# Masked stage: the two score products of a slot issued in turn; rotary stage: value products two units at a time instead of four

## The chip, the cores and the metric

The kernel runs on one core of a Trainium2 chip. The time is that of one execution on the device, in microseconds (us). A core has TensorE (matrix products, PE in the rows, with PEld for its weight loads), VectorE (DVE), ScalarE (ACT), GpSimd (POOL) and SyncE (SP, which issues the DMA transfers here). Each runs its own list of instructions in order and waits for the others by semaphores.

## The reference

Four attention layers, each followed by a small dense layer, on x of shape (4, 1024, 128), with 16 heads of 8 columns. Each layer gives one stage of the kernel, with 64 heads (4 batches x 16).

```
MASKED: q, k, v = norm(x) @ Wqkv + b;  p = softmax(q k^T / sqrt(8), keys >= query);  x += (p v) @ Wo + bo
RBF:    p = exp(-sigma * |k_i - q_j|^2), no softmax;                                 x += (p v) @ Wproj + b
REL:    softmax of (q k^T + relative positions, shifted) / sqrt(8);                  x += (p v) @ Wo + bo
ROPE:   q, k turned by their position (rotary);  softmax(q k^T / sqrt(8));           x += (p v) @ Wo + bo
after each: x += dense(norm(x))
```

For one head, p has 1024 x 1024 elements. The change touches the heads of MASKED and of ROPE.

## The kernel before

**Rounds and slots.** The kernel runs one round per head n, from n = -2 on. In round n two things are made side by side: the transposed scores S^T of head n (keys on the partitions, called kq), whose exponentials are needed for the values, and the scores S of head n + 2 (queries on the partitions, called qk), of which only the maximum of each row is wanted. A round has slots u = 0, 1, 2, ...; a slot makes one unit of each side, that is, up to four 128 x 128 tiles in one PSUM bank of 512 columns. `KQ_UNITS` and `QK_UNITS` name the tiles: a masked head has 9 units, since half of its tiles are hidden, a rotary head 16. A unit is a list of pieces (row tile, first column tile, tiles, place in the bank). In the masked stage the units of slots 3, 5 and 8 have two pieces on either side (3 + 1, 2 + 2 and 3 + 1 tiles), each with a tile on the diagonal; the others have one.

**The engines in a slot.** TensorE: `unit_kq` (its product is line 821 for MASKED and ROPE) and then `unit_qk` (line 866). The contraction has 51 rows on partitions 64 to 114 for kq and 48 rows on partitions 0 to 47 for qk, so each uses one half of the array's rows. In a diagonal tile two small products of 64 rows (line 826 for kq, `hide_kq`; line 871 for qk, `hide_qk`) add -1e30 to what is hidden; I call them masking steps. ScalarE takes the kq bank and writes its exponential into one of eight `probs` buffers (line 1043). VectorE reduces the qk bank to maxima `mx` (lines 1155 and 1166). Each side has three banks of `ring`: a kq product waits until the exponential of three units ago is out (`s_exp`), a qk product until the maxima of three items ago are (`s_sm`).

**The maximum's way.** After the last slot VectorE reduces `mx` to `mall` (line 1184), GpSimd splits it in three bf16 parts (lines 1401 to 1407), TensorE turns them (line 881, `turn_max`, after slot 3 of the masked rounds and slot 5 of the rotary ones), VectorE copies them to `mrow` (line 1194) and SyncE moves them to the rows of `qst` (line 616) that the next round's first kq product needs (`s_ldm`).

**Values.** `take_values` (line 909) multiplies the values with the exponentials of one unit into `ppv`, one f32 product for each tile, on a quarter of the array's columns; four tiles in different quarters run side by side. The trace shows two matmuls for each. `lag` says which units pass at which slot; slots past the end lie in the next round. A masked head passes three units at slots 5, 8 and 11, a rotary head four units at slots 5, 9, 13 and 17. The same rule serves the last two heads of the RBF stage.

**Fills.** In some rounds the TensorE list holds projections and transposes for the next batch or the end of the last one (`starts`, `finishes`, into `pm`, lines 925 to 995), at the slots that `Plan` sets. `Plan` isn't changed. Of the 64 rotary rounds 30 have fills; of the masked rounds 1 to 61, 37 run at the shortest interval.

Of the kernel before, what the change touches and what calls it, by code (L numbers as in the profile page):

```python
# [15 lines left out]
P = 128  # L16
NT = T // P
HALF = 512
SLOTS = 4
STAGES = 4  # L20
MASKED, RBF, REL, ROPE = range(STAGES)
HEADS = B * H
# [8 lines left out]
BASE = 6 * D  # L31
ROW = P // 2
# [30 lines left out]
def stage(n):  # L63
    return n // HEADS
# [11 lines left out]
def soft_index(n):  # L76

    return n - (HEADS if stage(n) > RBF else 0)
# [58 lines left out]
def loads_to(n):  # L137

    return 16 * sum(NLOAD[stage(m)] for m in range(n % SLOTS, n + 1, SLOTS))


def places_to(n):

    return 16 * sum(NPLACE[stage(m)] for m in range(n % SLOTS, n + 1, SLOTS))


def lag(rd):

    n = len(rd.kq)
    if rd.wide:  # L150
        return {u + 3: [u, u + 1] for u in range(0, n, 2)}
    if rd.s == REL:
        return {6: [0, 1, 2, 3, 4], 10: [5, 6, 7, 8], 14: [9, 10, 11, 12], 19: [13, 14, 15, 16, 17]}
    if n == 9:
        return {5: [0, 1, 2], 8: [3, 4, 5], 11: [6, 7, 8]}
    return {u + 5: [u, u + 1, u + 2, u + 3] for u in range(0, n, 4)}


def values_at(n, u):

    out = []
    if 0 < n <= LAST:
        out += [(n - 1, v) for v in lag(ROUNDS[n - 1]).get(u + ROUNDS[n - 1].slots, [])]
    if 0 <= n < LAST:
        out += [(n, v) for v in lag(ROUNDS[n]).get(u, []) if u < ROUNDS[n].slots]
    return out
# [203 lines left out]
def build(nc, a, k, out):  # L370
# [9 lines left out]
    with ctx:  # L380
        def sb(name, shape, dt=F32):
            return ctx.enter_context(nc.sbuf_tensor(name, shape, dt))

        def ps(name, shape):
            return ctx.enter_context(nc.psum_tensor(name, shape, F32))

        def sem(name):
            return ctx.enter_context(nc.semaphore(name))
# [56 lines left out]
        halves = sb("halves", [P, 2, P], BF16)  # L445
        hide_qk = sb("hide_qk", [P, 2, P], BF16)
        hide_kq = sb("hide_kq", [P, 2, P], BF16)
# [6 lines left out]
        ring = ps("ring", [P, 6, HALF])  # L454
# [9 lines left out]
        s_ld = [sem(f"s_ld{i}") for i in range(SLOTS)]  # L464
        s_ldm = [sem(f"s_ldm{i}") for i in range(SLOTS)]
        s_vs = [sem(f"s_vs{i}") for i in range(SLOTS)]
        s_os = [sem(f"s_os{i}") for i in range(SLOTS)]
        s_st = sem("s_st")
        s_exp = sem("s_exp")
        s_pv = sem("s_pv")  # L470
        s_ev = sem("s_ev")
        s_s = sem("s_s")
        s_sm = sem("s_sm")
# [29 lines left out]
        def rowset(s):  # L503

            return kst[s % 2], qst[s % 2]

        def bank_kq(rd, u):
            if rd.wide:
                y = 2 * (((rd.n - HEADS) * NT + u) % 3)
                return ring[:, y:y + 2]  # L510
            return ring[:, 3 + (rd.narrow + u) % 3]
# [257 lines left out]
        def _(pe):  # L769
# [60 lines left out]
            def unit_qk(rd, u):  # L830
# [41 lines left out]
                                               stop=end and h == 1)  # L872
                mm.then_inc(s_s, 1)

            def turn_max(rd):

                pe.wait_ge(s_mp, 4 * (soft_index(rd.n + 1) + 1))
                item = rd.turned()
                if item >= 3:
                    pe.wait_ge(s_sm, item - 2)  # L880
                pe.transpose(ring[:, item % 3].bitcast(BF16)[0:3 * NT, 0:P], mparts[:, (rd.n + 1) % 2].rearrange("p a t -> p (a t)"),
                             identb[:, :]).then_inc(s_s, 1)
# [89 lines left out]
            def finishes():  # L972

                for f in range(INTERVALS):
                    s, j = f // B, interval_of(f)
                    for h in range(2):
                        name = ("fill", j, f, "wo", h)
                        yield AT[name]
                        filled(name)
                        if s == RBF:  # L980
                            pe.wait_ge(s_ot, 64 * (f + 1))
                        else:
                            pe.wait_ge(s_at, soft_before(f) + 1)
                        for t in range(4):
                            q = (2 * t + h) * P
                            mm = pe.matmul(pm[:, t * P:(t + 1) * P], oT[:, q:q + P], wo[:, s], start=True, stop=True)  # L986
                        mm.then_inc(s_pf, 1)
                    yield from turn_norm(j, f, "f", f, "tf")
                    for h in range(2):
                        name = ("fill", j, f, "ff", h)  # L990
                        yield AT[name]
                        filled(name)
                        pe.wait_ge(s_wf, 2)
                        for t in range(4):
                            mm = pe.matmul(pm[:, t * P:(t + 1) * P], xnT[:, (4 * h + t) * P:(4 * h + t + 1) * P], wf[:, s // 2],  # L995
                                           start=True, stop=True)
                        mm.then_inc(s_pf, 1)
# [3 lines left out]
            start, finish = Steps(starts()), Steps(finishes())  # L1001
            start.go(-1)
            for rd in ROUNDS.values():
                if rd.n == 0:
                    pe.wait_ge(s_c1, NC1[0])
                for u in range(rd.slots):
                    if u < len(rd.kq):
                        unit_kq(rd, u)
                    if u < len(rd.qk):
                        unit_qk(rd, u)  # L1010
                    if u == rd.turn:
                        turn_max(rd)
                    for n, v in values_at(rd.n, u):
                        take_values(n, v)
                    start.go(rd.tick + u)
                    finish.go(rd.tick + u)
# [663 lines left out]
```

## Time and profile before

| | |
|---|---|
| median of 3 runs | 3001.47 us (3000.57 to 3001.97) |
| the profiled execution's own time | 2993.65 us |
| its span, first to last instruction | 2991.9 us |
| mean granted TensorE clock | 0.989 |
| busy: PE, PEld, DVE, ACT, POOL | 93%, 58%, 69%, 71%, 25% |
| chain that ended last | PE 74%, DVE 14%, ACT 4%, issue 4% |

The masked stage lies from about 70 to 602 us, RBF to 1127, REL to 2171, ROPE to 2950. Busy shares of TensorE count a matmul from its start to its modelled end, some 0.17 us after its last column went in, so rows that overlap are common: pace is read from start to start. "Idle before" in brackets is time in which the engine ran nothing, with what ended it.

### The profile page before, as it was taken

What the parts mean: (1) busy time and instruction counts of PE and PEld (TensorE: products, weight loads), DVE (VectorE), ACT (ScalarE), POOL (GpSimd) and SP (SyncE); (2) the same over time, 40 slices, a digit from 0 to 9 for tenths busy, and PEclk for the clock granted to TensorE, in tenths of its full rate; (3) what the DMA queues carried; (4) which work ended last, traced back from release to release, by engine and by line L of the source; (5) the groups of instructions that cost most, each with busy time, mean ns of one, the idle gap of its engine ahead of it and who ended that gap; (6) DMA issues with size and microseconds to landing.
All of it is one profiled execution on the core that took longest, in us unless ns stands there. A gap on an engine that the chain in (4) does not pass through costs nothing.

```text
span 2991.9 us, 106514 instructions
## 1 busy us (share of the span) xinstructions
PE 2779.5 (93%) x43980; PEld 1722.2 (58%) x44112; DVE 2076.9 (69%) x4755; ACT 2135.0 (71%) x3793; POOL 753.8 (25%) x1369
## 2 busy tenths in 40 slices
PE   4999999999999999999999999899988898888885
PEld 2677676755555556666666666566544444444443
DVE  3887787731221247777787777777789989889893
ACT  1676666789999986666666666566677777777773
POOL 3212222331312424401611440140032140231101
PEclk9999999999999999999999999999999999999997
DMA  5323232343323342311321231221113221132211
GB/s 173 96 78 112 79 110 74 111 137 94 114 80 118 96 134 63 114 47 52 103 66 47 69 110 47 68 76 56 37 53 94 61 80 57 55 94 60 75 52 31
DMA packets 195708, 244.78 MB, mean 82 GB/s; under 512 B 47044, under 2 KB 113220, under 8 KB 195224
## 3 DMA queue, kind: packets, MB, share of 16 engines
q1 hardware_dynamic: 195224, 237.96, 27.0%
q8 instruction: 349, 5.72, 0.8%
q14 instruction: 135, 1.11, 0.1%
HBM read 133.77 MB, written 100.14 MB: 78 GB/s over the span
## 4 chain that ended last, share of the span: by engine, by line
PE 74%; DVE 14%; ACT 4%; issue 4%; SPq 1%; DMA 1%; POOL 1%; ACTq 0%; DVEq 0%; POOLq 0%
PE ppv L909 30%; DVE mx L1166 9%; PE ring L821 8%; PE ring L810 6%; PE ring L859 5%; PE ring L794 5%; PE pm L941 3%; ACT probs L1043 3%; PE ring L866 3%; PE ring L826 2%; PE ring L850 2%; DVE seen L1161 1%; PE ring L871 1%; PE pm L986 1%; PE pm L995 1%
## 5 line engine op out<-in xcount | busy, mean ns | idle before, releaser
L1043 ACT ACTIVATE probs<-ring 128x512 f32<-128x512 f32 (+1 forms) x3280 | 1986.4, 697 | 787.8 <-PE ring L821 348.6
L1166 DVE TENSOR_REDUCE mx<-ring 128x1 f32<-128x512 f32 (+2 forms) x2112 | 1291.7, 649 | 287.0 <-PE ring L866 117.0
L909 PE MATMUL ppv<-probs,values 128*32 128x128 f32 x30208 | 1102.2, 277 | 5.6 <-DVE osb L1175 2.7
L909 PEld LDWEIGHTS ppv<-probs,values 128*32 128x32 f32 x30208 | 808.5, 110 | 245.3 <-issue 130.3
L866 PE MATMUL ring<-kst,qst 48*128 48x512 bf16 (+3 forms) x1792 | 563.1, 365 | 39.7 <-DMA kst<-records_k 20.6
L821 PE MATMUL ring<-qst,kst 51*128 51x512 bf16 (+4 forms) x1824 | 538.5, 362 | 37.0 <-ACT probs L1043 31.5
L1161 DVE CUSTOM_DVE_ANT_0 seen<-ring,low_seen 128x512 f32<-128x512 f32 x576 | 393.2, 683 | 138.1 <-PE ring L859 137.5
L1401 POOL CAST mparts<-mall 128x8 bf16<-128x8 f32 x192 | 36.7, 191 | 1310.2 <-DVE mall L1184 1303.1
L821 PEld LDWEIGHTS ring<-qst,kst 51*128 51x128 bf16 (+1 forms) x1824 | 137.3, 94 | 276.8 <-ACT probs L1043 171.6
L859 PE MATMUL ring<-kst,qst 112*128 112x512 bf16 (+3 forms) x768 | 251.0, 327 | 0.9 <-DVE mx L1166 0.9
L810 PE MATMUL ring<-qst,kst 115*128 115x512 bf16 (+3 forms) x768 | 250.6, 326 | 0.1
L866 PEld LDWEIGHTS ring<-kst,qst 48*128 48x128 bf16 x1792 | 145.6, 94 | 112.0 <-DVE mx L1166 57.2
L810 PE MATMUL ring<-qst_up,kst 115*128 115x512 bf16 (+3 forms) x640 | 205.0, 320 | 0.0
L859 PE MATMUL ring<-kst,qst_up 112*128 112x512 bf16 (+3 forms) x640 | 201.3, 315 | 2.4 <-DVE mx L1161 2.3
L1175 DVE COPY osb<-ppv 128x256 f32<-128x256 f32 x64 | 27.2, 424 | 238.3 <-PE ppv L909 238.3
L794 PE MATMUL ring<-qst,kst 54*128 54x512 bf16 x992 | 171.7, 385 | 0.0
L871 PE MATMUL ring<-hide_qk,halves 64*128 64x128 bf16 x1024 | 127.8, 220 | 0.0
L826 PE MATMUL ring<-hide_kq,halves 64*128 64x128 bf16 x1024 | 125.3, 217 | 0.0
L813 PE MATMUL ring<-low_kq,identb 128*128 128x129 bf16 (+2 forms) x576 | 123.8, 215 | 0.0
L826 PEld LDWEIGHTS ring<-hide_kq,halves 64*128 64x128 bf16 x1024 | 93.5, 96 | 41.2 <-issue 1.3
L810 PEld LDWEIGHTS ring<-qst_up,kst 115*128 115x128 bf16 x640 | 62.3, 97 | 89.1 <-issue 39.7
L810 PEld LDWEIGHTS ring<-qst,kst 115*128 115x128 bf16 x768 | 74.8, 97 | 52.6 <-issue 15.3
(143 smaller groups left out, 2687.2 us busy)
## 6 DMA issues: line engine op xcount, KB each, us to landing
qst<-records_q SPq DMA_DIRECT2D x448, 96.0 KB
heads_out<-osb SPq DMA_DIRECT2D x256, 128.0 KB, 1.9
kst<-records_k SPq DMA_DIRECT2D x320, 96.0 KB
records_k<-parts SPq DMA_DIRECT2D x96, 256.0 KB, 3.3
records_q<-parts SPq DMA_DIRECT2D x96, 256.0 KB, 3.5
kst<-records_k SPq DMA_DIRECT2D x128, 102.0 KB
oT<-heads_out SPq DMA_DIRECT2D x64, 128.0 KB, 2.7
den<-inverses SPq DMA_DIRECT2D x48, 128.0 KB, 2.6
```

The costliest lines, as they stand in the source:

```text
L794: mm = pe.matmul(bank[:, h], keys[rows, slot, kt * P:(kt + 1) * P], qs[rows, slot, h * HALF:(h + 1) * HALF], start=True, stop=True)
L810: mm = pe.matmul(bank[:, p0 - lo:p1 - lo], keys[rows, slot, kt * P:(kt + 1) * P], qq[rows, slot, p0:p1], start=p0 == lo, stop=p1 == hi and ...
L813: mm = pe.matmul(bank[:, m0 - lo:m1 - lo], identb[:, :], low_kq[:, m0 - first:m1 - first], start=False, stop=True)
L821: mm = pe.matmul(bank[:, at * P:(at + nt) * P], keys[rows, slot, kt * P:(kt + 1) * P], qs[rows, slot, q0 * P:(q0 + nt) * P], start=i == 0, ...
L826: mm = pe.matmul(bank[:, c:c + P], halves[half, h], hide_kq[half, h], start=False, stop=end and h == 1)
L859: mm = pe.matmul(bank[:, p0 - lo:p1 - lo], qq[rows, slot, qt * P:(qt + 1) * P], keys[rows, slot, p0:p1], start=p0 == lo, stop=p1 == hi)
L866: mm = pe.matmul(bank[:, at * P:(at + nt) * P], qs[rows, slot, qt * P:(qt + 1) * P], keys[rows, slot, k0 * P:(k0 + nt) * P], start=i == 0, ...
L871: mm = pe.matmul(bank[:, c:c + P], halves[half, h], hide_qk[half, h], start=False, stop=end and h == 1)
L909: mm = pe.matmul(ppv[32 * g:32 * g + 32, c:c + P], values[:, (n // H) % 2, v:v + 32], src[:, at * P:(at + 1) * P], start=u == 0 and qt < 4 ...
L1043: nc.scalar.activation(probs_of(rd.n, u), src, ACT.Exp, scale=1.0 if rd.s == RBF else SCALE).then_inc(s_exp, 1)
L1161: dve.tensor_tensor_reduce(seen[:, item % 3], bank[:, :], low_seen[:, first:first + HALF], 1.0, 3.0 * BIG, ALU.add, ALU.max, mx[:, slot, ( ...
L1166: ins = dve.tensor_reduce(mx[:, slot, to:to + 1], bank[:, at * P:(at + nt) * P], AX.X, ALU.max)
```

## The change

Two edits. First, in masked rounds 1 to 61 a new function `unit_both` takes the place of `unit_kq` and `unit_qk`: piece by piece it issues the kq product, then the qk product, then the masking steps of the two in turn. The waits are those of before; the wait for the qk bank (`s_sm`) stands between the first kq product and the first qk product. Second, `lag` for heads of 16 units passes units 0, 1 at slot 5, units 2, 3 at slot 6, and from unit 4 on the pair u, u + 1 at slot u + 4, so 8 passes of two units instead of 4 of four.

```
-    return {u + 5: [u, u + 1, u + 2, u + 3] for u in range(0, n, 4)}
+    return {5: [0, 1], 6: [2, 3], **{u + 4: [u, u + 1] for u in range(4, n, 2)}}
...
+            def unit_both(rd, u):
...
+                if u == 0:
+                    pe.wait_ge(s_ldm[n % SLOTS], places_to(n))
+                    pe.wait_ge(s_ld[m % SLOTS], loads_to(m))
+                if e >= 3:
+                    pe.wait_ge(s_exp, e - 2)
...
+                for i in range(max(len(rd.kq[u]), len(rd.qk[u]))):
+                    if i < len(rd.kq[u]):
...
+                        mm = pe.matmul(scores[:, at * P:(at + nt) * P], keys[ROW:ROW + BASE + 3, n % SLOTS, kt * P:(kt + 1) * P],
+                                       qs[ROW:ROW + BASE + 3, n % SLOTS, q0 * P:(q0 + nt) * P], start=i == 0, stop=end and not hidden)
...
+                    if i == 0 and item >= 3:
+                        pe.wait_ge(s_sm, item - 2)
+                    if i < len(rd.qk[u]):
...
+                        mm = pe.matmul(tops[:, to * P:(to + mt) * P], qs_m[0:BASE, m % SLOTS, qt * P:(qt + 1) * P],
+                                       keys_m[0:BASE, m % SLOTS, k0 * P:(k0 + mt) * P], start=i == 0, stop=end_m and not hidden_m)
...
+                    for h in range(2):
+                        if i < len(rd.kq[u]) and hidden:
+                            mm = pe.matmul(scores[:, c:c + P], halves[high, h], hide_kq[high, h], start=False, stop=end and h == 1)
...
+                        if i < len(rd.qk[u]) and hidden_m:
+                            mm = pe.matmul(tops[:, cm:cm + P], halves[low, h], hide_qk[low, h], start=False, stop=end_m and h == 1)
...
-                    if u < len(rd.kq):
-                        unit_kq(rd, u)
-                    if u < len(rd.qk):
-                        unit_qk(rd, u)
+                    if 0 < rd.n < HEADS - 2:
+                        unit_both(rd, u)
```

TensorE in a masked round, slot 3 and the turn of the maxima behind it. The rows name line, operation, output and inputs, and the output's size; `qst`, `kst` are the two operands, `ring` the banks. Before:

```order
L821 MATMUL ring<-qst,kst 128x384
L826 MATMUL ring<-hide_kq,halves 128x128 x2
L821 MATMUL ring<-qst,kst 128x128
L826 MATMUL ring<-hide_kq,halves 128x128 x2
L866 MATMUL ring<-kst,qst 128x384
L871 MATMUL ring<-hide_qk,halves 128x128 x2
L866 MATMUL ring<-kst,qst 128x128
L871 MATMUL ring<-hide_qk,halves 128x128 x2
L881 MATMUL ring<-identb,mparts 24x128
```

The same place in the changed kernel:

```order
L892 MATMUL ring<-qst,kst 128x384
L902 MATMUL ring<-kst,qst 128x384
L908 MATMUL ring<-hide_kq,halves 128x128
L912 MATMUL ring<-hide_qk,halves 128x128
L908 MATMUL ring<-hide_kq,halves 128x128
L912 MATMUL ring<-hide_qk,halves 128x128
L892 MATMUL ring<-qst,kst 128x128
L902 MATMUL ring<-kst,qst 128x128
L908 MATMUL ring<-hide_kq,halves 128x128
L912 MATMUL ring<-hide_qk,halves 128x128
L908 MATMUL ring<-hide_kq,halves 128x128
L912 MATMUL ring<-hide_qk,halves 128x128
```

The turn (L922) follows. The qk products moved up from behind all kq instructions to right behind the kq product of the same piece.

TensorE in a rotary round, from slot 5 with the turn to the next passes. Before, with four units (16 tiles) a pass:

```order
L821 MATMUL ring<-qst,kst 128x512
L866 MATMUL ring<-kst,qst 128x512
L881 MATMUL ring<-identb,mparts 24x128
L909 MATMUL ppv<-probs,values 32x128 x16
L821 MATMUL ring<-qst,kst 128x512
L866 MATMUL ring<-kst,qst 128x512
L821 MATMUL ring<-qst,kst 128x512
L866 MATMUL ring<-kst,qst 128x512
```

And in the changed kernel:

```order
L821 MATMUL ring<-qst,kst 128x512
L866 MATMUL ring<-kst,qst 128x512
L922 MATMUL ring<-identb,mparts 24x128
L950 MATMUL ppv<-probs,values 32x128 x8
L821 MATMUL ring<-qst,kst 128x512
L866 MATMUL ring<-kst,qst 128x512
L950 MATMUL ppv<-probs,values 32x128 x8
L821 MATMUL ring<-qst,kst 128x512
L866 MATMUL ring<-kst,qst 128x512
```

The pass of units 0 to 3 is cut in two, and slot 6's products moved between the halves; further on a pass stands behind every second slot. The lists of the other engines keep their order.

## Rows read from the trace of the kernel before

**Rows 1.** Windows, masked and rotary stage: us, busy by engine, clock, DMA

```profile
81.00:595.00 514.00, 505.04 (x8182) 358.77 (x8180) 408.42 (x921) 355.49 (x697) 133.84 (x313) 1.00 0.33 95
...
2171.00:2950.00 779.00, 687.91 (x10637) 368.45 (x10635) 671.97 (x1276) 594.94 (x1193) 172.36 (x336) 0.99 0.23 66
```

**Rows 2.** Timeline of TensorE, plain masked round: start, us, line, tiles, count

```profile
300.26 0.33 PE L821 MATMUL ring<-qst,kst 51*128 51x384 bf16 x1
...
300.51 0.33 PE L866 MATMUL ring<-kst,qst 48*128 48x384 bf16 x1
300.55 0.22 PE L821 MATMUL ring<-qst,kst 51*128 51x128 bf16 x1
...
301.06 0.23 PE L881 MATMUL ring<-identb,mparts 128*24 128x128 bf16 x1
...
301.98 0.28 PE L866 MATMUL ring<-kst,qst 48*128 48x256 bf16 x1
...
302.52 0.86 PE L909 MATMUL ppv<-probs,values 128*32 128x128 f32 x24
303.32 0.39 PE L821 MATMUL ring<-qst,kst 51*128 51x512 bf16 x1
```

**Rows 3.** The same timeline, slot 7 and the start of slot 8

```profile
303.55 0.38 PE L821 MATMUL ring<-qst,kst 51*128 51x512 bf16 x1
303.55 0.38 PE L866 MATMUL ring<-kst,qst 48*128 48x512 bf16 x1
303.76 0.22 PE L826 MATMUL ring<-hide_kq,halves 64*128 64x128 bf16 x1
...
303.88 0.32 PE L821 MATMUL ring<-qst,kst 51*128 51x384 bf16 x1
```

**Rows 4.** Timeline of VectorE, slot 3 of the same round

```profile
301.16 0.75 DVE L1166 TENSOR_REDUCE mx<-ring 128x1 f32<-128x384 f32 x2 [0.33 <-PE ring L871]
```

**Rows 5.** Waits of VectorE, 81 to 589 us: us in sum, times, longest

```profile
DVE mx L1166 <- PE ring L871: 64.4, 119, 1.9
DVE mx L1166 <- PE ring L866: 25.8, 62, 0.5
```

**Rows 6.** Windows: a plain masked, a plain rotary, a rotary round with projections

```profile
300.26:307.73 7.47, 7.47 (x131) 5.44 (x130) 6.17 (x14) 5.19 (x11) 0.78 (x4) 1.00 0.25 73
...
2330.23:2340.92 10.69, 9.73 (x165) 5.26 (x162) 10.12 (x19) 8.54 (x17) 0.78 (x4) 1.00 0.18 51
...
2400.30:2414.90 14.60, 12.67 (x141) 5.18 (x138) 9.63 (x17) 10.60 (x21) 0.96 (x5) 1.00 0.10 30
```

**Rows 7.** Timeline of VectorE, plain rotary round

```profile
2334.63 3.67 DVE L1166 TENSOR_REDUCE mx<-ring 128x1 f32<-128x512 f32 x6
2338.22 0.20 DVE L1194 COPY mrow<-ring 24x128 bf16<-24x128 bf16 x1
2338.85 3.82 DVE L1166 TENSOR_REDUCE mx<-ring 128x1 f32<-128x512 f32 x6 [0.42 <-PE ring L866]
```

**Rows 8.** Timeline of TensorE, same round: scores, values of four units, scores

```profile
2331.43 0.39 PE L866 MATMUL ring<-kst,qst 48*128 48x512 bf16 x1
2331.75 1.08 PE L909 MATMUL ppv<-probs,values 128*32 128x128 f32 x32
2332.76 0.39 PE L821 MATMUL ring<-qst,kst 51*128 51x512 bf16 x1
```

**Rows 9.** Timeline of TensorE, slot 5 of a masked round behind a transpose

```profile
219.42 0.27 PE L821 MATMUL ring<-qst,kst 51*128 51x256 bf16 x1
...
219.59 0.28 PE L866 MATMUL ring<-kst,qst 48*128 48x256 bf16 x1
```

**Rows 10.** Timeline of TensorE, rotary round with projections

```profile
2408.57 0.39 PE L821 MATMUL ring<-qst,kst 51*128 51x512 bf16 x1
...
2408.89 1.12 PE L941 MATMUL pm<-xnT,wkp 128*128 128x512 f32 x2
2409.95 0.39 PE L821 MATMUL ring<-qst,kst 51*128 51x512 bf16 x1
```

More of the change, by code:

```diff
@@ L873, in unit_qk @@
                 mm.then_inc(s_s, 1)
+            def unit_both(rd, u):
+                n, m = rd.n, rd.n + 2
+                e, item = rd.exps + u, rd.maxes + u + (0 <= rd.turn < u)
+                (keys, qs), (keys_m, qs_m) = rowset(stage(n)), rowset(stage(m))
+                if u == 0:
[3 more added lines that the diff above has]
+                    pe.wait_ge(s_exp, e - 2)
+                low, high = slice(0, ROW), slice(ROW, P)
+                scores, tops = bank_kq(rd, u), ring[:, item % 3]
+                for i in range(max(len(rd.kq[u]), len(rd.qk[u]))):
+                    if i < len(rd.kq[u]):
+                        kt, q0, nt, at = rd.kq[u][i]
+                        end, hidden = i == len(rd.kq[u]) - 1, q0 <= kt < q0 + nt
+                        c = (at + kt - q0) * P
+                        mm = pe.matmul(scores[:, at * P:(at + nt) * P], keys[ROW:ROW + BASE + 3, n % SLOTS, kt * P:(kt + 1) * P],
+                                       qs[ROW:ROW + BASE + 3, n % SLOTS, q0 * P:(q0 + nt) * P], start=i == 0, stop=end and not hidden)
+                        if end and not hidden:
+                            mm.then_inc(s_st, 1)
+                    if i == 0 and item >= 3:
+                        pe.wait_ge(s_sm, item - 2)
+                    if i < len(rd.qk[u]):
+                        qt, k0, mt, to = rd.qk[u][i]
+                        end_m, hidden_m = i == len(rd.qk[u]) - 1, k0 <= qt < k0 + mt
+                        cm = (to + qt - k0) * P
+                        mm = pe.matmul(tops[:, to * P:(to + mt) * P], qs_m[0:BASE, m % SLOTS, qt * P:(qt + 1) * P],
+                                       keys_m[0:BASE, m % SLOTS, k0 * P:(k0 + mt) * P], start=i == 0, stop=end_m and not hidden_m)
+                        if end_m and not hidden_m:
+                            mm.then_inc(s_s, 1)
+                    for h in range(2):
+                        if i < len(rd.kq[u]) and hidden:
+                            mm = pe.matmul(scores[:, c:c + P], halves[high, h], hide_kq[high, h], start=False, stop=end and h == 1)
+                            if end and h == 1:
+                                mm.then_inc(s_st, 1)
+                        if i < len(rd.qk[u]) and hidden_m:
+                            mm = pe.matmul(tops[:, cm:cm + P], halves[low, h], hide_qk[low, h], start=False, stop=end_m and h == 1)
+                            if end_m and h == 1:
+                                mm.then_inc(s_s, 1)
@@ L1006, in _ @@
                 for u in range(rd.slots):
-                    if u < len(rd.kq):
-                        unit_kq(rd, u)
-                    if u < len(rd.qk):
-                        unit_qk(rd, u)
+                    if 0 < rd.n < HEADS - 2:
+                        unit_both(rd, u)
+                    else:
+                        if u < len(rd.kq):
+                            unit_kq(rd, u)
+                        if u < len(rd.qk):
+                            unit_qk(rd, u)
                     if u == rd.turn:
```

## The prediction

> **What bounds the kernel now.** Read first the windows by stage [rows 1]: TensorE counts as busy for 505 of 514 us in the masked stage and for 688 of 779 us in the rotary stage. Matmul ends are modelled and each matmul's 0.2 us of latency is counted, so these shares say only that TensorE is hardly ever empty. What it does with the time is read from its timeline, start to start.
>
> A masked head without projection work takes 7.47 us: the 384-column product of slot 3 starts at 300.26 and again at 307.73, which is a window of [rows 6]. I call such a round plain. Its parts on TensorE follow without a hole, except one wait in slot 5. Score products use one half of the array each: S^T (kq) the upper 64 rows, S (qk) the lower 64. In slot 7 both run together: L821 and L866 start at 303.55, their two masking steps each from 303.76 on, and slot 8 starts at 303.88 [rows 3]; a paired masking step is thus 0.06 us. In slot 3 they don't: L821 starts at 300.26, but L866, which stands behind six kq instructions, at 300.51 [rows 2]. TensorE does look past some of them (the 128-column kq product, ahead of L866 in the order, starts at 300.55), yet not past all, and the lower half is empty for 0.25 us. VectorE stands idle in front of each of slots 0, 3 and 6, with 0.33 us before slot 3 [rows 4], and for 90 us in sum over 61 heads [rows 5]. So TensorE sets the pace of a plain masked round and VectorE has room.
>
> A plain rotary round is 10.69 us (window of 2330.23 to 2340.92), with VectorE at 10.12 us [rows 6]. Six row maxima in a row take 3.67 us, so the pitch is (3.67 - 0.68) / 5 = 0.598 us [rows 7]; 16 of them, a copy of 0.20 and a reduction and its gap of some 0.20 make 9.97 us. VectorE lacks 0.72 us per round: 0.42 behind the turned maximum [rows 7], and 0.1 us or so behind each of the other value passes, which the timeline merges into its runs (six maxima in 3.82 us instead of 3.67). All of them lie where TensorE runs a block of values of four units, 1.01 us from its start to the next score product (2331.75 to 2332.76) [rows 8].
>
> **The masked edit.** It changes the order of instructions on TensorE alone; none is added. Slot by slot:
> - Slots 0, 1, 2, 4, 6, 7 have one piece a side. Slot 0 keeps its order, and in slots 1 and 7 both halves are full already. Nothing.
> - Slot 3, and slot 8 of the same shape. Now: 0.25 (late start of qk) + 0.46 (384 columns 0.17, 128 columns 0.06, four masking steps 0.23) + 0.09 (change to the whole array for the turn) = 0.80, which is 300.26 to 301.06 [rows 2]. Then: both start together, 0.46 + 0.09 = 0.55. Saved: 0.25 us in each.
> - Slot 5. Its L866 starts at 301.98, 0.07 after VectorE has finished slot 3's maxima (301.16 + 0.75 = 301.91) [rows 2, 4]: it waits for that bank. This wait stays and now also holds the kq masking steps behind it. But VectorE started at 301.16 because slot 3's last qk masking step, L871, had ended (the releaser in its row), and that is 0.25 earlier afterwards. From L866 to the values it is 0.54 us, and the paired order needs no more. So the values of slot 5 come earlier by the 0.25 that slot 3 saved, and no second gain is there.
>
> A plain round is worth 0.25 + 0.25 = **0.50 us**. What is late next: VectorE starts slot 3 with 0.33 us of idle time before it [rows 4]; 0.08 is left. It is busy 6.17 of 7.47 us [rows 6], so 6.97 us still holds it. The kq result of slot 5 comes some 0.3 us later in its slot; ScalarE is busy 5.19 us of the round and no value pass needs slot 5 before slot 8. The load for the next head and the maximum's way over GpSimd keep their order; their distances shrink by 0.25 us.
>
> The edit holds in 61 heads. Going by the intervals from one slot 3 to the next, 37 are plain: 37 x 0.50 = 18.5 us. In 11 TensorE does projections or transposes and waits for nobody; there slot 5 has no wait, and its qk product starts 0.17 late (219.42 and 219.59) [rows 9], so 0.25 + 0.25 + 0.17 = 0.67 each, 7.4 us. In the other 13 a wait for ScalarE, a transfer or VectorE's squares is on the path and takes half of it: 13 x 0.2 = 2.6 us. Together **28 us**, bounds 15 (VectorE or the waits take half) and 33.
>
> The Trainium skill, "TensorE: Matmul & The Clock Gate", Part 3, says that matmuls are strictly first in, first out and only weight loads are pulled ahead. The trace differs: L866 at 300.51 runs before kq steps that stand ahead of it. By the page's rule slot 3 would have taken 2 x 0.46 + 0.09 = 1.01 us and the edit would give 0.46 per slot; the row has 0.80, and the sum goes by the row.
>
> **The rotary edit.** Before, units 0 to 3 pass at slot 5, then four units every four slots; after, two units at slots 5 and 6 and then every two slots. 64 heads, and the last two of the Gaussian stage, which I leave at nothing. The newest unit of a pass is then 3 slots old (4 at slot 5) instead of 2, so no pass waits longer for its exponential.
> - Price: a value block costs more than its matmuls. Three units take 0.80 (302.52 to 303.32) [rows 2] and four 1.01 [rows 8], so a unit is 0.21 and the block 0.16 on top; entering it costs 0.1 (L866 at 2331.43, values at 2331.75, with 0.22 of columns) [rows 8]. Two units take 0.58. Eight blocks instead of four: 4 x 0.26 = 1.04 us more of TensorE per head.
> - Gain: the longest stretch without scores falls from 1.01 to 0.58.
> In a plain round TensorE's own work is 16 x 0.22 = 3.5 for score pairs, 16 x 0.21 = 3.4 for values, now 4 x 0.26 = 1.0 and then 2.1, and 0.2 for the turn: 8.1 and then 9.2 us, under VectorE's 9.97. So the price is hidden behind VectorE, and the 0.42 of idle time behind the turn is covered by the 0.43 that the block is shorter. Between 0 and 0.72 I take 0.35, half, since TensorE then has only 0.8 us to spare and every pair still waits for two engines. 32 plain rounds x 0.35 = **11 us** saved.
> The other 32 heads: in two no maxima are computed, nothing counted. In 30 there are projections; around 2408 values, scores and a projection of 1.06 us follow each other with no wait [rows 10]. There each extra block costs its 0.26, up to 1.04 per head. But the window of such a round has TensorE busy only 12.67 of 14.60 us [rows 6]; the rest is waits for ScalarE and banks, which shorter blocks fill. I take 0.1 lost per head, **3 us**, bounds 30 lost and 10 won.
>
> **Sum.** 2993.65 (the profiled execution's own time, 1.75 more than its span) - 28 - 11 + 3 = 2957.7. The median of the runs is 3001.47, 7.8 above; with it, 2965.5.
>
> **Rivals.**
> - Rotary neutral or worse (0.12): TensorE paces the 30 fill rounds, which lose most of 1.04 us each, and the plain rounds gain nothing or little: -28 + 20 = -8, 2993. For it: [rows 10] without a hole. Against: the 1.9 us of waits in such a round.
> - VectorE takes over the masked rounds (0.13): 0.08 us of room before slot 3 is thin; if it isn't there, a plain round gains only 0.25: -15 - 11 + 3 = -23, 2978.
> - More (0.08): the rotary rounds reach VectorE's floor (32 x 0.72 = 23) and the fill rounds gain 8: -28 - 23 - 8 = -59, 2942.
> - Slower (0.07): the extra block changes pace the whole rotary stage. It decides once TensorE's sum passes VectorE's 9.97 us, that is, if a block change costs over 0.36 instead of 0.26. Then 64 rounds pay 1.04 or more: +67 - 28 = +39, 3040. Against it: two independent block lengths give the same 0.16.
> - The edits not in effect (under 0.01): the order on TensorE shows both.
>
> **How the numbers follow.** The forecast, 2965.5, has 0.60; masked 20 to 33 us and rotary 0 to 18 us give 2950 to 2981. With the rivals on either side in part, the range is 2945 to 2990. A measurement of this kernel can't tell 0.2% (6 us) from no change. Faster by more: 0.60 + 0.13 + 0.08 and half of the first rival, 0.86. Within: the other half and small remains, 0.07. Slower: 0.07.
>
> **What would show it.** In the trace after: both 384-column products of slots 3 and 8 start together; a plain masked round of 6.97 us (7.2 means VectorE, 7.47 nothing won); slot 5's qk product still starts just after slot 3's maxima. A plain rotary round of 10.3 us, eight value blocks of 0.58 with no idle time of VectorE behind the turn; fill rounds within 0.3 us of now. Wrong would be: pairs that start together and yet last longer than 0.06 a step, or rotary rounds above 10.69.

## The result: 1.4% faster

The changed kernel takes 2960.91 us (median of 4 executions, 2954.58 to 2967.66). The kernel before took 3001.72 us beside it. The ratio is 0.9862, with a 95% interval of 0.9832 to 0.9893. The predicted 2965.5 us lies 4.6 us above the measured median. The profiled execution took 2954.58 us (its span is 2952.8), 39.07 less than that of before. Of the executions behind the figures further below, two, one of the late turn (3661.42 us, mean granted clock 0.659) and one of the kernel before beside the last kernel (3495.26 us, 0.730), lie hundreds of us above all others and are left out of the medians and ratios.

Measured from the end of the first exponential of each stage's first head to that of the next stage (in the rotary stage to the end of its last exponential), these 39 us lie as follows (us, profiled executions):

| stage | before | after | difference | of it, by kind of round |
|---|---|---|---|---|
| masked | 532.4 | 510.5 | -21.9 | 37 plain -15.3, 11 fill rounds -6.5, 13 others -0.6, first round +0.5 |
| Gaussian | 524.2 | 524.5 | +0.3 | its last round +0.3 |
| relative | 1044.3 | 1047.7 | +3.4 | its first round +0.5, the rest in rounds with projections and transfers |
| rotary | 778.6 | 757.8 | -20.8 | 32 plain -13.5, 30 fill rounds -5.9, last two -1.4 |

A stage's sum holds to about 3 us only: stages that an edit leaves alone move by that much from one profile to the next (next section).

First the windows of the trace after: the masked and the rotary stage, a plain masked round and a plain rotary one (columns as in [rows 1] and [rows 6]: length, then busy us of TensorE, its weight loads, VectorE, ScalarE, GpSimd, then clock and DMA).

```profile
81.00:567.00 486.00, 458.85 (x8086) 307.99 (x8085) 407.23 (x912) 350.16 (x687) 130.66 (x307) 0.99 0.34 99
2130.00:2910.00 780.00, 721.62 (x10895) 344.40 (x10886) 682.51 (x1300) 624.31 (x1217) 173.24 (x341) 0.99 0.22 67
268.94:275.95 7.01, 6.71 (x130) 4.58 (x130) 6.16 (x14) 5.17 (x11) 0.78 (x4) 1.00 0.56 157
2324.05:2334.32 10.27, 9.76 (x165) 4.63 (x162) 10.03 (x19) 8.86 (x17) 0.78 (x4) 1.00 0.19 56
```

The masked round is 7.01 us where it was 7.47, the rotary one 10.27 where it was 10.69 [rows 6]. VectorE has the same work in both (6.16 and 6.17 us; 10.03 and 10.12 us): it stands idle for less.

TensorE's timeline of slots 3 to 5, the counterpart of [rows 2]:

```profile
268.94 0.33 PE L892 MATMUL ring<-qst,kst 51*128 51x384 bf16 x1
268.94 0.33 PE L902 MATMUL ring<-kst,qst 48*128 48x384 bf16 x1
...
269.34 0.21 PE L912 MATMUL ring<-hide_qk,halves 64*128 64x128 bf16 x1
269.49 0.23 PE L922 MATMUL ring<-identb,mparts 128*24 128x128 bf16 x1
...
269.87 0.27 PE L892 MATMUL ring<-qst,kst 51*128 51x256 bf16 x1
270.44 0.28 PE L902 MATMUL ring<-kst,qst 48*128 48x256 bf16 x1 [0.30 <-DVE mx L1210]
...
270.99 0.86 PE L950 MATMUL ppv<-probs,values 128*32 128x128 f32 x24
```

Both products of slot 3 start at 268.94, and the turn follows after 0.55 us, where it was 0.80. Slot 5's S product still waits, now by 0.30 us, for VectorE's maxima of slot 3. These are the three instructions of VectorE before that wait ends, the last of slot 2 and both of slot 3 (compare [rows 4]):

```profile
268.82 0.68 DVE L1210 TENSOR_REDUCE mx<-ring 128x1 f32<-128x512 f32 x1
269.62 0.56 DVE L1210 TENSOR_REDUCE mx<-ring 128x1 f32<-128x384 f32 x1
270.10 0.28 DVE L1210 TENSOR_REDUCE mx<-ring 128x1 f32<-128x128 f32 x1
```

VectorE ends slot 2 at 269.50 and starts slot 3 at 269.62. The 0.33 us of idle time before slot 3 are 0.12 now. Slot 3's maxima start 0.68 us after its products, where it was 0.90 (301.16 - 300.26 in [rows 4] and [rows 2]), so they come 0.22 earlier in the slot. TensorE alone would have made it 0.25: from the last masking step's modelled end (269.34 + 0.21) to the reduction it is 0.07 us. Slot 8 takes 0.54 us from its first product to the values behind it:

```profile
272.34 0.32 PE L892 MATMUL ring<-qst,kst 51*128 51x384 bf16 x1
272.34 0.32 PE L902 MATMUL ring<-kst,qst 48*128 48x384 bf16 x1
...
272.88 1.28 PE L950 MATMUL ppv<-probs,values 128*32 128x128 f32 x24
```

In the kernel before it was 0.78, from the 303.88 of [rows 3] to

```profile
304.66 1.28 PE L909 MATMUL ppv<-probs,values 128*32 128x128 f32 x24
```

VectorE's waits for scores in the masked stage (us in sum, times, longest) are 65 us in the lines that answer to [rows 5], where they were 90:

```profile
DVE mx L1210 <- PE ring L912: 40.3, 78, 2.0
DVE mx L1210 <- PE ring L902: 24.6, 62, 0.5
```

In the plain rotary round (VectorE's timeline, as in [rows 7]) only one idle stretch of 0.20 us is left behind the turned maximum:

```profile
2327.68 0.20 DVE L1238 COPY mrow<-ring 24x128 bf16<-24x128 bf16 x1
2327.88 0.69 DVE L1210 TENSOR_REDUCE mx<-ring 128x1 f32<-128x512 f32 x1
2328.78 5.47 DVE L1210 TENSOR_REDUCE mx<-ring 128x1 f32<-128x512 f32 x9 [0.20 <-PE ring L866]
```

Nine maxima in 5.47 us are a pitch of (5.47 - 0.68) / 8 = 0.599 us: VectorE's own, without a gap. TensorE, on the other side, now waits for VectorE twice around the turn, before the S product of slot 5 and before the turn itself (its timeline):

```profile
2324.35 0.65 PE L950 MATMUL ppv<-probs,values 128*32 128x128 f32 x16
2324.93 0.39 PE L821 MATMUL ring<-qst,kst 51*128 51x512 bf16 x1
...
2326.03 0.39 PE L866 MATMUL ring<-kst,qst 48*128 48x512 bf16 x1 [0.21 <-DVE mx L1210]
2326.72 0.22 PE L922 MATMUL ring<-identb,mparts 128*24 128x128 bf16 x1 [0.30 <-DVE mx L1210]
```

A block of two units is 0.58 us from its start to the next scores (2324.35 to 2324.93), as predicted.

### The profile page after: what moved, and what is told of

It reads as the page before. It is cut to its first block, busy times and chain, and to the rows that moved or that the text cites. A ratio compares the mean times of both kernels' runs of the same rounds, so it can differ in the third digit from the quotient of the medians.

```text
span 2952.8 us, 106453 instructions
## 1 busy us (share of the span) xinstructions
PE 2754.6 (93%) x43980; PEld 1641.9 (56%) x44112; DVE 2073.6 (70%) x4755; ACT 2150.1 (73%) x3793; POOL 753.2 (26%) x1369
## 4 chain that ended last, share of the span: by engine, by line
PE 68%; DVE 20%; issue 5%; ACT 3%; SPq 1%; DMA 1%; POOL 1%; ACTq 0%; DVEq 0%; POOLq 0%
PE ppv L950 28%; DVE mx L1210 15%; PE ring L810 6%; PE ring L859 6%; PE ring L794 5%; PE ring L821 3%; PE ring L892 3%; PE pm L982 3%; PE ring L850 2%; DVE seen L1205 1%; ACT probs L1087 1%; PE pm L1027 1%; PE ring L908 1%; PE pm L1036 1%; ACT xn L1095 1%
## 5 line engine op out<-in xcount | busy, mean ns | idle before, releaser
L950 PE MATMUL ppv<-probs,values 128*32 128x128 f32 x30208 | 1156.9, 278 | 5.6 <-DVE osb L1219 2.7
L950 PEld LDWEIGHTS ppv<-probs,values 128*32 128x32 f32 x30208 | 791.9, 110 | 334.0 <-issue 181.3
L866 PE MATMUL ring<-kst,qst 48*128 48x512 bf16 (+1 forms) x1060 | 366.3, 391 | 43.1 <-DVE mx L1210 21.4
L821 PE MATMUL ring<-qst,kst 51*128 51x512 bf16 (+2 forms) x1092 | 346.6, 385 | 3.6 <-ACT probs L1087 3.0
L902 PE MATMUL ring<-kst,qst 48*128 48x512 bf16 x732 | 210.5, 330 | 16.5 <-DVE mx L1210 16.5
L892 PE MATMUL ring<-qst,kst 51*128 51x512 bf16 x732 | 203.6, 329 | 3.7 <-DMA qst<-mrow 3.7
L1219 DVE COPY osb<-ppv 128x256 f32<-128x256 f32 x64 | 27.2, 424 | 238.7 <-PE ppv L950 238.7
L866 PEld LDWEIGHTS ring<-kst,qst 48*128 48x128 bf16 x1060 | 90.8, 94 | 122.5 <-DVE mx L1210 76.6
L821 PEld LDWEIGHTS ring<-qst,kst 51*128 51x128 bf16 (+1 forms) x1092 | 70.9, 94 | 138.3 <-ACT probs L1087 95.8
L912 PE MATMUL ring<-hide_qk,halves 64*128 64x128 bf16 x976 | 118.6, 216 | 0.0
```

The lines of the kernel that those rows point to most:

```text
L821: mm = pe.matmul(bank[:, at * P:(at + nt) * P], keys[rows, slot, kt * P:(kt + 1) * P], qs[rows, slot, q0 * P:(q0 + nt) * P], start=i == 0, ...
L866: mm = pe.matmul(bank[:, at * P:(at + nt) * P], qs[rows, slot, qt * P:(qt + 1) * P], keys[rows, slot, k0 * P:(k0 + nt) * P], start=i == 0, ...
L892: mm = pe.matmul(scores[:, at * P:(at + nt) * P], keys[ROW:ROW + BASE + 3, n % SLOTS, kt * P:(kt + 1) * P], qs[ROW:ROW + BASE + 3, n % SLO ...
L902: mm = pe.matmul(tops[:, to * P:(to + mt) * P], qs_m[0:BASE, m % SLOTS, qt * P:(qt + 1) * P], keys_m[0:BASE, m % SLOTS, k0 * P:(k0 + mt) * ...
L950: mm = pe.matmul(ppv[32 * g:32 * g + 32, c:c + P], values[:, (n // H) % 2, v:v + 32], src[:, at * P:(at + 1) * P], start=u == 0 and qt < 4 ...
```

## The experiments

Eleven kernels ran. All diffs are against the changed kernel. Stage and round times come from each kernel's profiled execution, by the ends of the heads' first exponentials, as in the table above; "plain round" is the median over the plain ones. Ratios are to the kernel before, on the same chip; the changed kernel's is 0.9862 (0.9832 to 0.9893).

### The two edits apart

The masked edit alone, rotary passes as before:

```
-    return {5: [0, 1], 6: [2, 3], **{u + 4: [u, u + 1] for u in range(4, n, 2)}}
+    return {u + 5: [u, u + 1, u + 2, u + 3] for u in range(0, n, 4)}
```

> The masked edit alone; the rotary stage passes four units at a time as before. My reading (each edit works in its own stage): the masked stage loses 22 us and the rotary stage keeps 778.6 us, so about 2971 us profiled, 22 below the kernel before. Rival (the masked edit is worth less alone, part of the gain is a shift of work between the stages): less than 15 us. In the profile a plain masked round of 7.02 us and a plain rotary round of 10.69 us.

Measured: 2969.86 us, ratio 0.9896 (0.9879 to 0.9913). Plain masked round 7.02 us, plain rotary round 10.70; rounds 127 and 128 take 15.5 and 14.6 us as before, where the changed kernel has 15.8 and 15.1.

The rotary edit alone:

```
-                    if 0 < rd.n < HEADS - 2:
+                    if False:
```

> The rotary edit alone; masked slots as before. My reading: masked stage 532 us as before, rotary stage 758 us, so 21 us below the kernel before, 32 plain rounds giving 13.5 us, the two last rounds 1.5 us and the rounds with projections 6 us. Rival (rotary neutral, block changes eat it): within 6 us of the kernel before. In the profile plain rotary rounds of 10.27 us.

Measured: 2990.02 us, ratio 0.9948 (0.9927 to 0.9969). Plain masked round 7.46 us, plain rotary 10.27. The two ratios multiply to 0.9845, and the changed kernel has 0.9862: **the edits add**, within the intervals. Each plain round moves with its own edit alone. The stage sums are less sharp. The masked edit alone left the masked stage at 507.5 us and the rotary stage, whose order it doesn't touch, at 775.4, where before has 778.6; the rotary edit alone has 529.8 us for the untouched masked stage (532.4 before) and 761.4 for the rotary one. The median with the rotary edit alone is 13.8 us below the kernel before beside it and not the 21 expected; its executions spread from 2978.70 to 3000.79 us, and the profiled one, the longest, ran 54 us at half clock (last section).

### What gates slot 5

The prediction said that slot 5's wait for VectorE stays and that slot 5's own pairing is worth nothing in a plain round, but 0.17 us in a fill round. Slot 5 as before, the rest paired:

```
-                    if 0 < rd.n < HEADS - 2:
+                    if 0 < rd.n < HEADS - 2 and u != 5:
```

> The changed kernel, but slot 5 of the masked rounds issues all kq products first and then the qk products, as before. My reading (in a plain round slot 5 waits for VectorE to finish slot 3's maxima, whatever the order): plain masked rounds stay at 7.02 us within 0.03; the 11 rounds with a projection lose 0.1 to 0.17 us each. Rival (the paired order in slot 5 carries part of the gain): plain rounds at 7.15 or more. A second rival (the pairing holds slot 5's masking steps back behind the wait and costs): plain rounds below 6.99.

Measured: plain masked round 7.017 us, which is unchanged; the 11 fill rounds 108.8 us in sum, where the changed kernel has 106.9. That is 0.17 each on average (0.15 to 0.19), the upper end of what was expected. The total of one execution (2968.19 us) says little: 23.9 us of it ran at half clock (last section).

Then a part of VectorE's work in front of that wait is left out: the second maximum of slot 3 (128 columns, 0.28 us, of which 0.20 lie behind the end of the first). The row maxima of one tile are missing from the result.

```
-                    for qt, k0, nt, at in unit:
+                    for qt, k0, nt, at in unit[:1] if u == 3 and stage(n) == MASKED and n > 2 else unit:
```

> The changed kernel, but VectorE leaves out the 128-column maximum of slot 3 (one tile's row maxima are not computed), 0.28 us less work per masked round, for heads 3 to 63. My reading (VectorE gates slot 5, and this gate is what the masked edit runs into): slot 5's qk product starts up to 0.2 us earlier and a plain masked round takes 6.8 us. Rival (TensorE alone sets the round, VectorE's time is hidden): 7.02 us as without it.

Measured: plain masked round 6.820 us, 0.197 less; the stage 498.9 us. The 11 fill rounds, in which slot 5 waits for nobody, stayed at 106.9 us. VectorE stands idle for parts of every round, 6.16 of 7.01 us being busy, and still 0.2 us less of it shortens the round by 0.2. It isn't the bound by its sum, but **slot 3's maxima are on the path** of a plain round.

### Slot 8

```
-                    if 0 < rd.n < HEADS - 2:
+                    if 0 < rd.n < HEADS - 2 and u != 8:
```

> The changed kernel with slot 8 of every round issued as before (all of the S^T product's steps, then the S product's). Theory: TensorE paces the end of the masked round, so slot 8 takes 0.78 us instead of 0.54 and a plain masked round 7.26 us; the stage is 61 x 0.24 = 15 us longer at most and 9 at least (the plain rounds alone). Rival (VectorE paces the whole round since the edit): 7.02 to 7.08 us.

Measured: plain masked round 7.255 us, 0.237 more, and each of the 11 fill rounds 0.24 more; the stage 519.0 us, 8.5 more, just short of the least expected (9), its first round being 1.3 us shorter here. TensorE's timeline in slot 8 shows the old stagger:

```profile
269.73 0.32 PE L821 MATMUL ring<-qst,kst 51*128 51x384 bf16 x1
...
269.96 0.33 PE L866 MATMUL ring<-kst,qst 48*128 48x384 bf16 x1
270.00 0.22 PE L821 MATMUL ring<-qst,kst 51*128 51x128 bf16 x1
...
270.50 1.28 PE L950 MATMUL ppv<-probs,values 128*32 128x128 f32 x24
```

Slot 8 takes 0.77 us here and 0.54 paired. Its gain is TensorE's own and arrives whole. No kernel has slot 3 apart: what is left of the plain round's 0.44 us is 0.20.

### The place of the turn

Slot 5 waits because the S banks go round in three and the turn, at slot 3, takes one of them: slot 5's bank is the one that slot 3 filled. With the turn behind slot 5, slot 5 gets the bank of slot 2, and the turn itself has to wait for slot 3's maxima. The same number also moves VectorE's copy of the turned maxima and SyncE's load of them by two slots.

```
-TURN_SLOT = [3, 0, 6, 5]
+TURN_SLOT = [5, 0, 6, 5]
```

> The changed kernel, with the turned maximum of the masked rounds behind slot 5 instead of slot 3. Slot 5's qk product then no longer waits for slot 3's maxima, since one item fewer stands between them. My reading (VectorE's gate costs a plain masked round up to 0.4 us): 6.6 to 6.85 us per plain round, 6 to 15 us in all. Rival (the later copy of the maxima makes the next round's first kq product wait for its transfer, which takes 2 us from the copy): plain rounds of 7.0 us or more, with waits of L892 for qst<-mrow.

Measured: 2953.99 us (median of four executions), ratio 0.9833 (0.9811 to 0.9855), which can't be told from the changed kernel's; plain masked round 6.687 us, 0.33 less than the changed kernel; the stage 496.4 us, 14.1 less. Of these, 11.6 us lie in the 37 plain rounds and 3.6 in the stage's first round: it took 9.8 to 11.6 us in the ten kernels with the turn at slot 3 and 7.7 to 8.5 in the three with a later turn, and why wasn't looked into. The 13 rounds that are neither plain nor fill rounds took 1.8 more. TensorE's timeline, slot 5 and the turn, then slot 8 and the next slot 0:

```profile
262.57 0.27 PE L892 MATMUL ring<-qst,kst 51*128 51x256 bf16 x1
262.57 0.27 PE L902 MATMUL ring<-kst,qst 48*128 48x256 bf16 x1
...
263.48 0.21 PE L922 MATMUL ring<-identb,mparts 128*24 128x128 bf16 x1 [0.31 <-DVE mx L1210]
263.61 0.86 PE L950 MATMUL ppv<-probs,values 128*32 128x128 f32 x24
...
264.96 0.32 PE L892 MATMUL ring<-qst,kst 51*128 51x384 bf16 x1
...
265.50 1.28 PE L950 MATMUL ppv<-probs,values 128*32 128x128 f32 x24
266.72 0.39 PE L892 MATMUL ring<-qst,kst 51*128 51x512 bf16 x1
```

Slot 5's products start together. A wait of 0.31 us remains, but it stands behind slot 5's scores and no longer ahead of them. The price shows in the waits of the first S^T product of a round for the load of the maxima (us in sum, times, longest), of its weights (PEld) and of the product itself (PE). First the changed kernel, then this one:

```profile
PEld ring L892 <- DMA qst<-mrow: 4.2, 2, 2.3
PE ring L892 <- DMA qst<-mrow: 3.7, 2, 2.0
```

```profile
PEld ring L892 <- DMA qst<-mrow: 15.1, 45, 2.2
PE ring L892 <- DMA qst<-mrow: 5.4, 6, 1.9
```

The weights' 2 waits have become 45, the product's 2 have become 6: the load now lands just in time. The two rows lie over each other in time and don't add. One slot later still:

```
-TURN_SLOT = [3, 0, 6, 5]
+TURN_SLOT = [6, 0, 6, 5]
```

> The changed kernel with the turn of the maxima in the masked rounds at slot 6, two slots of one piece after slot 5's bank. Theory: at slot 5 the turn still waits 0.3 us for VectorE in each round, but its result then reaches the next head's operands just in time (waits for the load of the maxima, 20 us in sum). One slot later the first is smaller and the second larger: plain masked rounds 6.7 to 7.0 us, and the waits of the first S^T product for the load grow beyond 20 us. Rival (the load has slack, the turn's wait is what is left): 6.4 to 6.6 us.

Measured: 2969.12 us (one execution); plain masked round 7.26 us, beyond the upper end of what I had expected; the stage 522.0 us. The same two waits:

```profile
PEld ring L892 <- DMA qst<-mrow: 27.8, 47, 1.9
PE ring L892 <- DMA qst<-mrow: 15.8, 45, 1.6
```

They grew, as the theory had it: the weights' by 12.7 us over 61 rounds, 0.21 each, and 45 products wait where 6 did. The round lost 0.57. The rest is in slot 8: slot 6, the turn and slot 7 have the three banks ahead of it, so it waits for slot 6's maximum as slot 5 did for slot 3's (TensorE's timeline of this kernel):

```profile
270.00 0.32 PE L892 MATMUL ring<-qst,kst 51*128 51x384 bf16 x1
...
270.46 0.33 PE L902 MATMUL ring<-kst,qst 48*128 48x384 bf16 x1
...
271.01 1.28 PE L950 MATMUL ppv<-probs,values 128*32 128x128 f32 x24
272.58 0.39 PE L892 MATMUL ring<-qst,kst 51*128 51x512 bf16 x1 [0.29 <-DMA qst<-mrow]
```

The S product starts 0.46 us behind its partner. In this round slot 8 takes 1.01 us to its values (270.00 to 271.01), where the turn at slot 5 has 0.54 (264.96 to 265.50), and from there to the next slot 0 it is 1.57 us, where it was 1.22. That is 0.47 for slot 8's bank and 0.35 for the load, and 0.24 us are saved ahead of slot 8. So the late turn pays at slot 5 and no longer at slot 6.

### The price of a value block

Rotary units from 4 on passed one at a time, 14 blocks in a head instead of 8:

```
-    return {5: [0, 1], 6: [2, 3], **{u + 4: [u, u + 1] for u in range(4, n, 2)}}
+    return {5: [0, 1], 6: [2, 3], **{u + 3: [u] for u in range(4, n)}}
```

> The changed kernel, with the rotary heads passing one unit at a time from unit 4 on: 14 blocks a head instead of 8. My reading (each block costs 0.26 us more of TensorE, 9.2 us of work in a plain round now, then 10.8, over VectorE's 9.97): a plain rotary round of 10.7 to 11.0 us, the rounds with projections 1.0 to 1.6 us longer each. Rival (the block change is hidden, only the length of a block counts): 10.0 to 10.27 us.

Measured: 3009.63 us (one execution); the rotary stage 812.1 us, plain rotary round 11.03. The 30 fill rounds took 0.8 us more each, less than the 1.0 to 1.6 expected and than six blocks at 0.25 us, so a part of the price is hidden there. From unit 4 on, TensorE's timeline is a row of equal steps:

```profile
2314.40 0.42 PE L950 MATMUL ppv<-probs,values 128*32 128x128 f32 x8
2314.76 0.39 PE L821 MATMUL ring<-qst,kst 51*128 51x512 bf16 x1
2314.76 0.39 PE L866 MATMUL ring<-kst,qst 48*128 48x512 bf16 x1
2315.08 0.43 PE L950 MATMUL ppv<-probs,values 128*32 128x128 f32 x8
...
2315.76 0.43 PE L950 MATMUL ppv<-probs,values 128*32 128x128 f32 x8
```

The step is 0.68 us. A score pair is 0.22 and a unit of values 0.21, so **a block costs 0.25 us beyond its matmuls**; the prediction had 0.26. In this stretch TensorE sets the pace, since VectorE's own pitch is 0.60. The price is real; at eight blocks it is hidden.

Only the first pass of four split in two, the later ones left at four units (five blocks):

```
-    return {5: [0, 1], 6: [2, 3], **{u + 4: [u, u + 1] for u in range(4, n, 2)}}
+    return {5: [0, 1], 6: [2, 3], **{u + 5: [u, u + 1, u + 2, u + 3] for u in range(4, n, 4)}}
```

> The changed kernel, with only the first pass of a rotary head split (units 0, 1 at slot 5 and 2, 3 at slot 6) and the others of four units as before: 5 blocks. My reading (0.3 of the 0.42 us gained in a plain round is the idle time of VectorE behind the turn): 10.35 to 10.45 us, with gaps of 0.13 us left behind the blocks of four. Rival (the shorter blocks later in the round bring it): 10.6 us or more.

Measured: 2961.4 us (one execution); plain rotary round 10.42 us. Of the 0.42 us that the plain round gained, 0.28 come from splitting the pass that stands at the turn and 0.15 from the other three. So the idle time behind the turn was the larger part, and the small gaps of about 0.1 us behind the other blocks were real too. Rounds 127 and 128 are as before here (15.5 and 14.6 us), although their first pass is split as well.

### The last Gaussian heads, and two further edits together

The prediction left rounds 127 and 128, in which those two narrow heads' values pass, at nothing; they take 0.8 us more. With their passes of four units back:

```
+    if rd.s == RBF:
+        return {u + 5: [u, u + 1, u + 2, u + 3] for u in range(0, n, 4)}
     return {5: [0, 1], 6: [2, 3], **{u + 4: [u, u + 1] for u in range(4, n, 2)}}
```

> The changed kernel, but the last two heads of the RBF stage pass four units at a time as before; the rotary heads keep two. My reading: in these two rounds block changes are paid with nothing to hide them, and in some executions (seen in two profiles, granted clock 0.5 from about 1090 us on, 24 and 55 us long) TensorE's clock stays at half there; with passes of four the rounds go back to 15.52 and 14.57 us (-0.8 us) and the executions with a long half-clock stretch get rare, so a median of 2953 to 2956 us and a spread under 8 us. Rival (the half-clock stretch has nothing to do with these passes): median and spread as in the changed kernel, 2955 to 2968.

Measured: 2955.19 us, ratio 0.9851 (0.9833 to 0.9869). The two rounds are back at 15.5 and 14.6 us, where the changed kernel has 15.8 and 15.1. The ratio can't be told from the changed kernel's. The expected spread under 8 us didn't come (2953.07 to 2964.13), so nothing shows that these passes bring the half clock.

The late turn and this edit together:

```
-TURN_SLOT = [3, 0, 6, 5]
+TURN_SLOT = [5, 0, 6, 5]
+    if rd.s == RBF:
+        return {u + 5: [u, u + 1, u + 2, u + 3] for u in range(0, n, 4)}
```

> The changed kernel with two edits together: the turn of the maxima in the masked rounds at slot 5 instead of slot 3, and the narrow Gaussian heads back to passes of four units. If the two gains add: plain masked rounds 6.69 us, rounds 127 and 128 back at 15.5 and 14.6 us, the masked stage about 497 us, the rest of the trace as in the changed kernel. Against the changed kernel 37 x 0.33 = 12 us plus 0.8, so some 2947 to 2949 in the median where the changed kernel has 2961. If the shorter masked rounds are given back elsewhere (the wait for the maxima's load at the head of a round), only half of it.

Measured: **2944.35 us, ratio 0.9822 (0.9799 to 0.9844)**. Plain masked round 6.70 us, masked stage 496.4 us, rounds 127 and 128 15.5 and 14.6 us. By the ratio that is 0.40% under the changed kernel (12 us), as summed; the two intervals overlap by a little, so the ratios alone don't settle it. The plain masked rounds, 0.32 to 0.33 us shorter in both traces with the turn at slot 5, are the firmer evidence.

## Why the prediction was right, and where its terms were off

The direction, the main mechanisms and the bounds held. Term by term:

- **Plain masked round**: 0.50 predicted, 0.44 measured. Slot 8 gave 0.24 of 0.25. Slot 3 gave 0.22 of 0.25 at the place that counts, the start of its maxima, since these begin 0.07 us behind the last masking step and not 0.04. The mechanism was right in both slots: slot 5 apart changed nothing in plain rounds, slot 8 apart cost 0.24, and 0.2 us less of slot 3's maxima gave 0.2. Slot 3's own share was read from the trace and not tested by a kernel. The claim that VectorE keeps a little room before slot 3 held as well (0.12 us is left, 0.08 was predicted); the rival in which it takes over didn't happen.
- **Masked fill rounds**: 0.67 each predicted, 0.59 measured (6.5 us of 7.4), the same small loss in slots 3 and 8. The 0.17 of slot 5 was met to the digit.
- **The 13 other masked rounds**: 2.6 us predicted, 0.6 measured. The term for them was a guess, and they aren't of one kind. In six (18, 34, 41, 50, 54 and 58) 0.24 us arrived in each, what one slot gives, near the half that the sum took; round 2 gave 0.1 and round 38 nothing. The other five (32, 33, 48, 49 and 52) differ from profile to profile: 48.0 and 46.6 us in sum in the two kernels with the masked slots as before, 47.2 to 48.9 in the five with the changed kernel's masked order. So their change, 0.9 us longer in the profiled pair, can't be told from scatter. What they wait for wasn't taken apart.
- Together the masked stage gave 21.9 us where 28 were forecast, inside the bounds of 15 to 33.
- **Plain rotary round**: 0.35 predicted, 0.42 measured (13.5 us of the predicted 11). TensorE's price of four more blocks was hidden, as argued. VectorE's floor of 9.97 us is 0.30 away.
- **Rotary fill rounds**: 3 us lost predicted, 5.9 gained in these two profiles. Part of that is scatter: these 30 rounds took 417.3 and 413.9 us in the two profiles with passes of four, and 410.9 to 415.4 (mean 412.9) in the nine with passes of two. So the gain, taken by the means, is 2.7 us (415.6 - 412.9), and anything from a loss of 1.5 to a gain of 6.4 by the single ones. Behind it stand rounds of both signs that are the same in nearly every profile. Rounds 195, 211 and 227 are 0.77 us longer (14.61 to 15.38), rounds 200, 216 and 232 0.56 shorter (13.89 to 13.33). Both effects that the prediction named are there, a price and a filling of waits; the 0.1 us lost per head gave their sum the wrong sign.
- **The last two rotary rounds and the last Gaussian heads**: both were left at nothing. The first gave 1.4 us, 0.4 of it with the first pass split alone and the rest with the others; the second cost 0.8 us. Splitting only the first pass costs nothing there, so it is the later blocks of two; why they aren't hidden wasn't looked into.
- The relative stage took 3.4 us more. Its heads pass their values as before, and 0.5 us belongs to round 128. The thirteen profiles have this stage at 1044.3 to 1049.5 us, the masked edit alone at 1044.6 and the late turn at 1045.9, both with the changed kernel's order in this stage, but for round 128 in the first. I take the rest for scatter; it wasn't tested by itself.

The good total owes something to errors that cancel: the masked stage was 6 us too high, the rotary stage 13 us too low (20.8 instead of 8), and 3.7 us went elsewhere. The sum was -36 and the profiles gave -39.

That the median lies only 4.6 us from the forecast is luck as well. The four executions fall in two groups, 2954.58 and 2954.92 us at a mean granted clock of 0.989 and 0.988, 2966.90 and 2967.66 at 0.983 and 0.982. Their median is the middle of a gap of 12 us, and the prediction, which set the median 7.8 us above the profiled execution, knew nothing of it. One sum of the chances is off by a little: 0.60 + 0.13 + 0.08 and half of 0.12 make 0.87 and not 0.86.

In the rows with slot 8 apart, the S product starts at 269.96 and the 128-column S^T product, which the program has ahead of it, at 270.00. The Trainium skill, "TensorE: Matmul & The Clock Gate", Part 3, has matmuls strictly first in, first out; these rows contradict it, as [rows 2] did.

## What to carry to other kernels

Where two products use different halves of the array, issue them piece by piece in turn: a product that stands behind several instructions for the other half starts late (0.25 us here), and each such slot on TensorE's path is worth that. In a ring of buffers, look at who takes a buffer between two users of the same kind: moving one small step (the turn) behind the waiting product gave 0.33 us a round, more than pairing gave in a slot, until the result of that step came too late for its own consumer. Splitting long blocks helps while the price (0.25 us a block) fits under the engine that sets the pace; count it per round before, and don't put rounds that wait for other engines into the sum with one figure: here some kept what a slot gave, and others moved either way.

## What the runs showed of the hardware

In the changed kernel's profile the granted clock of TensorE is at its full level, 2.4 GHz, in nearly every stretch from the first heads to the last, with single stretches of 3.4 or 6.8 us at half; behind the last head it is at half (0.50 from 2920 to 2952 us). In rounds 126 and 127, where the Gaussian stage turns into the relative one, it falls for longer in some executions. Windows of the kernel with the rotary edit alone (TensorE's granted clock is the third number from the end): 20 us before the fall, 48 us within it, 20 us behind it.

```profile
1074.00:1094.00 20.00, 18.52 (x364) 11.37 (x356) 2.93 (x6) 18.29 (x21) 0.72 (x2) 1.00 0.34 106
...
1100.00:1148.00 48.00, 46.71 (x322) 16.68 (x326) 22.06 (x51) 16.70 (x29) 1.39 (x7) 0.50 0.07 20
1150.00:1170.00 20.00, 18.50 (x279) 12.26 (x282) 19.14 (x62) 13.53 (x27) 6.03 (x13) 1.00 0.25 69
```

At half clock, 1.2 GHz, these two rounds take 27.4 and 27.2 us, where the changed kernel has 16.3 and 15.8. TensorE was busy for 18.52 of the 20 us before the fall, but most of its idle time stands right ahead of it, where round 126 begins and waits for ScalarE. The first row is the kernel with the rotary edit alone, the second the changed kernel:

```profile
1093.26 0.37 PE L821 MATMUL ring<-qst,kst 54*128 54x512 bf16 x1 [1.28 <-ACT probs L1087]
```

```profile
1072.51 0.37 PE L821 MATMUL ring<-qst,kst 54*128 54x512 bf16 x1 [1.28 <-ACT probs L1087]
```

The wait is the same 1.28 us in both, and the clock fell only behind the first (0.54 from 1094 to 1100 us, where the changed kernel has 1.00 from 1075 to 1081). So this wait alone doesn't bring the fall; whether it takes part in it isn't shown. In the profiles of the kernels with slot 5 apart and with the late turn the stretch is 23.9 us long, in those of before and of the changed kernel there is none at that place. The kernel with the late turn and the Gaussian passes of four has 13.7 us of it (its round 126 takes 22.15 us), and the one with the first pass split alone 3.4. So it comes without passes of two in the last Gaussian heads as well. Such a stretch of 54 us costs (27.4 - 16.3) + (27.2 - 15.8) = 22.5 us, as much as one of the edits gives; that is why the plain rounds' times, the same within 0.01 us in every profile with the same order, were the better measure for each part. What sets it off stays open.
